# Attention and routed experts on one core: loads of x group by group, ones by a memset, a third group normed on VectorE, a later clear

## What is computed

```python
xn = _layernorm(x, axis=-1)
x = x + _L0_attn_ref(xn, Wqkv, Wproj, bproj) + _L0_ffn_ref(xn, gate_w, gate_b, w1, b1, w2, b2)
# attention: 16 heads of 8, rotary q and k, causal within a window of 64, softmax, times v, projected
# experts: gates = xn @ gate_w.T + gate_b; the 2 best of 8, softmax over the two;
#          gelu(xn @ w1[e] + b1[e]) @ w2[e] + b2[e], weighted
```

## Time and profile before

| | us |
|---|---|
| median of 3 runs | 841.19 (840.72 to 841.76) |
| the profiled execution | 844.36 |
| its span | 842.5 |
| mean granted clock of TensorE | 0.943 of full speed |

### The profile page before, as it was taken

The page is one execution under the profiler, slowest core; times in us unless marked ns, Lnnn a source line. Parts: engine busy times, 40 slices in busy tenths (PEclk is TensorE's granted clock), DMA queues, the critical chain, the costliest instruction groups (busy, mean ns, idle before and its releaser), DMA issues.

```text
span 842.5 us, 26905 instructions
## 1 busy us (share of the span) xinstructions
PE 696.1 (83%) x10234; PEld 541.9 (64%) x10238; DVE 493.3 (59%) x1382; ACT 359.2 (43%) x681; POOL 408.4 (48%) x566
## 2 busy tenths in 40 slices
PE   6567888767877778778777979999999999998776
PEld 3455666545555545545554669899998988986554
DVE  6589877886556656556545834444444444454764
ACT  1435764424344433344334533444343434444443
POOL 2675331015555555545554135666666655664334
PEclk9899998879999999899989989999999999999987
DMA  9587767344564745654664777888888877883878
GB/s 259 148 204 198 174 155 185 90 136 131 153 175 133 192 124 132 158 153 122 153 167 122 184 195 217 221 232 225 229 229 219 213 212 218 223 228 94 231 237 249
DMA packets 213079, 154.15 MB, mean 183 GB/s; under 512 B 32560, under 2 KB 192944, under 8 KB 212952
## 3 DMA queue, kind: packets, MB, share of 16 engines
q1 hardware_dynamic: 199032, 131.41, 60.6%
q0 software_dynamic: 8640, 17.97, 6.2%
q10 hardware_dynamic: 5280, 3.06, 1.3%
HBM read 97.93 MB, written 54.34 MB: 181 GB/s over the span
## 4 chain that ended last, share of the span: by engine, by line
PE 24%; DVE 21%; issue 19%; DMA 10%; another core or an unknown queue 8%; POOL 7%; SPq 7%; ACT 2%; ACTq 0%; DVEq 0%; POOLq 0%
DVE mx L885 8%; POOL chosen_y L1135 6%; PE ps L614 4%; DMA chosen_y<-xn,to 4%; PE ps L561 3%; DMA xn<-in_b 3%; PE ps L554 2%; SPq L352 2%; PE ps L665 2%; PE ps L678 2%; PE ps L598 2%; POOL xn L1146 1%; PE ps L642 1%; PE ps L591 1%
## 5 line engine op out<-in xcount | busy, mean ns | idle before, releaser
L885 DVE TENSOR_REDUCE mx<-ps 128x8 f32<-128x1024 f32 x128 | 156.6, 1223 | 145.9 <-remote 74.2
L1053 ACT ACTIVATE PT<-ps 128x1024 f32<-128x1024 f32 x128 | 131.0, 1023 | 236.7 <-PE ps L598 199.0
L1129 POOL DMA_INDIRECT slots_x<-xn,pos x128 | 126.5, 988 | 130.6 <-DVE mx L885 96.1
L1074 ACT ACTIVATE hb<-ps,b1b 128x256 f32<-128x256 f32 x284 | 116.5, 470 | 162.6 <-issue 93.3
L1135 POOL DMA_INDIRECT chosen_y<-xn,to x142 | 137.9, 971 | 48.9 <-issue 30.3
L678 PEld LDWEIGHTS ps<-xn,hb 128*128 128x128 f32 x1136 | 138.4, 192 | 3.7
L678 PE MATMUL ps<-xn,hb 128*128 128x128 f32 x1136 | 138.5, 275 | 0.0
L665 PE MATMUL ps<-xn 128*128 128x256 f32 x568 | 136.1, 383 | 0.0
L614 PE MATMUL ps<-PT,V 128*32 128x64 f32 (+1 forms) x3072 | 104.6, 258 | 16.2 <-issue 11.2
L665 PEld LDWEIGHTS ps<-xn 128*128 128x128 f32 x568 | 103.5, 192 | 11.4
L937 DVE TENSOR_TENSOR to<-eq,cf_s 128x2 int32<-128x2 f32 x71 | 11.9, 168 | 135.6 <-DMA chosen_y<-xn,to 97.8
(11 more groups left out here) (130 smaller groups left out, 931.1 us busy)
## 6 DMA issues: line engine op xcount, KB each, us to landing
xn<-in_w SPq DMA_DIRECT2D x142, 256.0 KB
QK<-stack SPq DMA_DIRECT2D x128, 192.0 KB
stack<-sp SPq DMA_DIRECT2D x64, 192.0 KB
xn<-slots_x SPq DMA_DIRECT2D x71, 132.0 KB
stack<-sp SPq DMA_DIRECT2D x64, 128.0 KB
xn<-chosen_y SPq DMA_DIRECT2D x32, 256.0 KB, 4.3
xn<-in_b SPq DMA_DIRECT2D x71, 64.0 KB
stack<-sp SPq DMA_DIRECT2D x64, 64.0 KB
```

The source lines that it names most:

```text
L885: e.tensor_reduce(mo[:, :, :, c, t], ps[:, 0:2, :].rearrange("p g (h k) -> p g h k", k=P), AX.X, ALU.max, negate=True).then_inc(v_mx, 1)
L1053: e.activation(PT[:, u % 2, :], ps[:, 2:4, :].rearrange("p c k -> p (c k)"), ACT.Exp, scale=SCALE).then_inc(a_exp, 1)
L1074: e.activation(hb[:, s, c, :], ps[:, 2 * s + c // 2, (c % 2) * SL:(c % 2 + 1) * SL], ACT.Gelu, bias=b1b[:, i % NW, c:c + 1]).then_inc(a_ge ...
L1129: e.indirect_dma_start(out=Xs, out_offset=bass.IndirectOffsetOnAxis(ap=pos[:, n, u:u + 1], axis=0), in_=xn[:, u, :], in_offset=None).then_ ...
```

## The change

The first four loads of x are issued at the start, the others one by one, group 4 + k at q = -22 + 4 k, and SP issues them where the list says. The clear goes from the front to q = -12. The ones are no longer copied by SP: GpSimd sets the whole k half of `QK` (four buffers of 2048 bf16 per partition) to 1.0 by a memset before its cast, and the first reads into `QK` and the first transposed scores wait for that. The loads of the weights are put in another order, the values' and the gate's weights with a semaphore of their own, the bias with another, for which the gate's addition now waits. Group 2 is normed wholly on VectorE, as groups 0 and 1.

```diff
-    order = [("warm", 16), ("clear",)]
+    order = [("warm", 16)] + [("xload", g) for g in range(4)]
...
-        for g in range(2, NG):
+        for g in range(3, NG):
             d = FIRST + 4 * (g - 1) - q
             order.extend(("apply", g, j) for j, at in enumerate((4, 3, 2, 2, 1, 0)) if d == at)
-        if q == FIRST + 3:
-            order.append(("ones",))
+        if q - FIRST in range(0, 4 * (NG - 4), 4):
+            order.append(("xload", 4 + (q - FIRST) // 4))
+        if q == FIRST + 10:
+            order.append(("clear",))
...
         @block.sync
-            for g in range(NG):
-                e.dma_start(xr[:, GR[g]:GR[g + 1], :], xv[:, GR[g]:GR[g + 1], :]).then_inc(d_x[g], 16)
             for what, *a in ORDER:
-                if what == "ones":
-                    e.wait_ge(p_cb, 1)
-                    for n in range(NQ):
-                        for g in range(2):
-                            e.dma_start(QK[64 * g + 48:64 * g + 51, n, 1, :].rearrange("p (r c) -> p r c", c=P),
-                                        onesb[0:3, :].unsqueeze(1).broadcast_to((3, 16, P))).then_inc(d_one, 16)
+                if what == "xload":
+                    g = a[0]
+                    e.dma_start(xr[:, GR[g]:GR[g + 1], :], xv[:, GR[g]:GR[g + 1], :]).then_inc(d_x[g], 16)
...
                     if b >= NQ:
                         e.wait_ge(e_st, 4 * (b - NQ) + 4)
+                    else:
+                        e.wait_ge(p_init, 4)
...
         @block.tensor
-                    e.wait_ge(d_q, LOADS_Q)
+                    e.wait_ge(d_q, 16)
...
-                        e.wait_ge(d_one, 32 * NQ)
+                        e.wait_ge(p_init, 4)
...
         @block.vector
-                    if g >= 2:
+                    if g >= 3:
                         continue
...
-                    e.wait_ge(d_q, LOADS_Q)
+                    e.wait_ge(d_wv, LOADS_WV)
...
                     e.wait_ge(e_vg, n + 1)
+                    e.wait_ge(d_gb, 16)
...
         @block.scalar
+            e.dma_start(wv_f, wqkv[:, 256:384]).then_inc(d_wv, 16)
+            e.dma_start(gw_s[:], gate_w).then_inc(d_wv, 16)
             e.dma_start(wq_s[:], wqkv[:, 0:256]).then_inc(d_q, 16)
-            e.dma_start(wv_f, wqkv[:, 256:384]).then_inc(d_q, 16)
-            e.dma_start(gw_s[:], gate_w).then_inc(d_q, 16)
-            e.dma_start(gb_s[:], gate_b.partition_broadcast(P)).then_inc(d_q, 16)
+            e.dma_start(gb_s[:], gate_b.partition_broadcast(P)).then_inc(d_gb, 16)
...
         @block.gpsimd
             e.memset(ones8[:], 1.0).then_inc(p_init, 1)
+
+            e.memset(QK[:, :, 1, :], 1.0).then_inc(p_init, 1)
             e.wait_ge(d_cb, 16)
             e.tensor_copy(cb_s[:], cb_f).then_inc(p_cb, 1)
...
-                if what == "norm" and a[0] >= 2:
+                if what == "norm" and a[0] >= 3:
```

More of the change, by code:

```diff
@@ L286, in attention_moe_kernel @@
         d_g = [semaphore(f"d_g{i}") for i in range(NF)]
-        d_o, d_one = semaphore("d_o"), semaphore("d_one")
+        d_o, d_wv, d_gb = semaphore("d_o"), semaphore("d_wv"), semaphore("d_gb")
         e_xt, e_vg, e_rt, e_qk, e_qt, e_sc, e_mt, e_st = (semaphore("e_" + n) for n in (
@@ L308, in attention_moe_kernel @@
         block = ctx.enter_context(nc.Block())
-        LOADS_Q = 4 * 16
+        LOADS_WV = 2 * 16
         LOADS_C = 16
@@ L323, in xn_ready @@
         def xn_ready(u):
-            if u < GR[2]:
+            if u < GR[3]:
                 return v_xn, u + 1
-            g, j = divmod(u - GR[2], 6)
+            g, j = divmod(u - GR[3], 6)
             return (p_xn, 3 * g + ON_POOL.index(j) + 1) if j in ON_POOL else (a_xn, 3 * g + ON_ACT.index(j) + 1)
@@ L979, in _ @@
                     g, u = a[0], GR[a[0]] + a[1]
-                    e.wait_ge(p_nrm, PNRM * (g - 1))
+                    e.wait_ge(p_nrm, PNRM * (g - 2))
                     e.activation(xn[:, u, 0:P], xr[:, u, :], ACT.Identity, bias=nb[:, u:u + 1],
@@ L1091, in _ @@
                     n1, n2 = nb[:, u0:u1], mv[:, u0:u1, 0]
-                    k = PNRM * (g - 2)
-                    e.wait_ge(v_nrm, 24 + 3 * (g - 1))
+                    k = PNRM * (g - 3)
+                    e.wait_ge(v_nrm, 36 + 3 * (g - 2))
                     for _ in range(3):
@@ L1123, in _ @@
                         e.wait_ge(d_z, 16 * (1 + NE))
-                        e.wait_ge(v_xn, GR[2])
-                        e.wait_ge(a_xn, (NT - GR[2]) // 2)
-                        e.wait_ge(p_xn, (NT - GR[2]) // 2)
+                        e.wait_ge(v_xn, GR[3])
+                        e.wait_ge(a_xn, (NT - GR[3]) // 2)
+                        e.wait_ge(p_xn, (NT - GR[3]) // 2)
                     if n == 0 or u % 2:
```

## The result

| | before | changed |
|---|---|---|
| median, four runs each | 841.48 us (840.72 to 842.35) | 852.52 us (849.52 to 857.58) |
| the profiled execution | 844.36 us | 854.76 us |
| its span | 842.5 us | 852.9 us |
| mean granted clock of TensorE | 0.943 | 0.925 |

The ratio is 1.0137, with an interval of 1.0081 to 1.0193: slower, by 11.0 us where the prediction had 5.0. 852.5 lies outside the range of 839.0 to 848.4. The sign and the first half of the mechanism were right; the size was not.

The account below looks back on a forecast made before the run. The prediction took the start to be bound by a chain of waits, then VectorE's work. The turn's +3.2 us and the clear's +1.8 gave +5.0 on 841.19, so 846.2 us, with an 8-in-10 range of 839.0 to 848.4.

Parts of the forecast that it names:

- The gap of 3.9 us: Before the first rotated q and k turn: VectorE ready 3.9 us before the queued values' store landed, the most winnable there.
- Memset held in full: At group 0's first guess: GpSimd's memset, 6.9 us by elements, holds VectorE's step until it ends, +4.66 us.
- Rivals 1 to 3: At VectorE's group-0 step: memset holds nobody, clear hidden, 839.3 (0.17); likewise, clear paid, 841.1 (0.13); memset by bytes, 842.7/840.9 (0.12).
- The cast: On GpSimd directly behind the memset: falls into group 0's norm, +0.82 us, and no longer stalls group 1's, -0.50.
- The 1.38 us: In VectorE's start: its wait for the gate's bias goes, worth 0 to 1.38 us.
- Third group, 3.34 us: Ahead of the rotation of q and k: norming group 2 on VectorE adds 3.34 us; GpSimd and ScalarE end no wait.
- The turn: TensorE's first turn of rotated q and k, forecast to start near 29.95 instead of 26.79, +3.2 us.
- From there the order is that of before: From the turn to the first scores: same steps wait for SP, ScalarE and GpSimd, so nothing is added.
- the spread loads of x: On SP's queue: loads of groups 4 to 10, one per four steps, land in time; cost 0, bound 1 us.
- The clear, +1.8: At step -12, ahead of pair 1's write: the clear delays scores 4 by 1.8 us, bounds 0 and 3.9.
- Carried through: Behind the start: a microsecond lost or won before 48 us reaches the end, since every engine runs one fixed order.
- The sum: Over the whole kernel: 3.2 us at the turn plus 1.8 for the clear, +5.0 us.

Follow-up runs that it names:

- e8: Changed kernel with the memset as half as many f32 elements, put first, and the clear behind the store of values 1; 759.44 us, ratio 1.0000.
- e2: Kernel before with only the GpSimd memset of QK in place of SP's copied ones; 759.12 us, ratio 1.0023.
- e4: Changed kernel with group 2's Newton rounds and rows back on GpSimd and ScalarE; 762.51 us, ratio 1.0056.
- e6: Changed kernel with the memset as 4096 f32 elements, put first on GpSimd, and V's clearing moved behind the cast; 760.22 us, ratio 1.0013.
- e9: Changed kernel with short early memset, early clear, group 2 on GpSimd and ScalarE (its row later), zero products, x loads reordered; 754.74 us, ratio 0.9947.
- e10: Kernel before with loads of x in parts, weights' loads reordered and the clear behind the store of values 1; 758.47 us, ratio 1.0009.
- e3: Changed kernel with the clear issued behind the store of values 1 instead of at step -12; 763.33 us, ratio 1.0042.
- e11: Kernel before with loads of x in parts, weights' loads reordered and the clear at step -12; 759.08 us, ratio 1.0005.
- e5: Changed kernel with twelve products of zeros in TensorE's gap before the turn; 765.35 us, ratio 1.0086.

## Why the prediction was right or wrong

**The gap of 3.9 us.** Right for the changed kernel: with the queue short its turn follows VectorE's sum, and once the memset is out of the way it comes at 24.85 (e8), 1.9 us before the old one with a group more on VectorE. What the text did not see is that 3.9 us is VectorE's reserve alone: while GpSimd norms group 2, ScalarE's way to the same turn had only 1.6 (e2, e4).

**Memset held in full.** Right, in mechanism and size: the memset took 6.92 us against 6.9, the held step 4.68 against some 4.8. It moves what follows by 4.51 us; the sum's 4.66 counts the step's own 0.17 once too often. The Trainium skill, "SBUF — State Buffer", Who interferes with whom, counts any GpSimd instruction against a VectorE one that uses both ports; this trace agrees, for an instruction that only writes, with 4.68 us where 0.17 is usual. "VectorE: DVE Perf Modes" (Trainium skill), Zero memsets, states the count by elements for VectorE; of GpSimd the runs here show the same, 6.92 us for 8192 and 3.51 for 4096 elements of equal bytes. Rivals 1 to 3 fall with these rows. The 0.87 ns an element that the prediction gives the cast is not in its row: 0.82 us for 768 elements are 1.07. That the cost would vanish with an earlier, shorter memset was not in the text, and was worth 4.5 us at the turn (e6).

**The cast, and the weights.** Nearly: 0.82 was forecast, 0.63 came (1.74 less 1.11), but through the late landing of the constants and not from its place behind the memset. The 1.38 us were counted as gone only in the rivals, rightly, as in the held case the wait lay under the hold.

**Third group, 3.34 us.** The row was read rightly, the counterpart was not: the text says that GpSimd and ScalarE end no wait in the new order, but with group 2 left to them ScalarE's L981 would stand in front of the values' copy (e4: 1.2 to 1.3 us net). It doesn't enter the sum for the kernel as changed, where VectorE paid all of it. What the text lacked is its echo at the routing.

**The turn.** +2.68 us against +3.2.

**"From there the order is that of before".** This step failed. The order was that of before, the time of two of its parts was not: in the changed kernel's first profile 2.7 us were added between the turn and the first scores. 2.1 of them lie in front of the read of pair 0, where TensorE was granted 0.50; the other 0.7 are the read itself, 6.3 to 7.1 us from its issue to the scores in every trace with a load of x right in front of it, and 5.9 and 5.5 in before and e2. The prediction had the spread loads of x at 0 (bound 1 us); why the read takes longer isn't shown, since it took 6.2 and 6.6 in e9, where that load is gone. I had the granted clock of before in the earlier trace rows (0.66 and 0.74 in the start, 1.00 from 40 to 50 us) and treated it as a constant of the stage. In the changed kernel TensorE stands idle for all of 24 to 28 us (0.00 busy, before 1.21) and comes back at 0.50, where it stays to 36 (the kernel before comes back at 0.50 too, and has 0.74 from 28 to 32). It would be easy to call that the cause. The other traces don't bear it out as a rule: from 20 to 40 us e10, whose turn came after 4.97 us of idling, had 0.68, and the kernel before, with 6.72 us of idling, 0.83; the changed kernel itself had 0.57, 0.83 and 0.57 in its three profiles. Shown is what a low grant costs there, about 2 us at the first maxima (53.5 and 53.7 against 51.6, and the two groups of the sixteen traces), and that the changed kernel met it in two of three profiles; why, isn't.

**The clear, +1.8.** Right in place and nearly in size: 2.1 us in the changed kernel's marks (+5.4 to +7.5), 2.3 to 2.6 by e3, 1.3 by e11 against e10.

**Carried through.** Right to scores 28 (+7.9 from 8 to 28). Behind it the routing adds 1.5 us (+9.4 at scores 32), which no part of the prediction had; and the end has +10.4.

**The sum.** By its own steps: 2.68 (turn) + 2.06 (clock) + 0.66 (read) + 2.15 (clear) + 0.35 (from scores 4 to 28) + 1.50 (routing) + 1.00 (behind scores 32) = 10.4 us of span, against 5.0. On the two other chips the same kernel costs 4.5 and 7.4 us. The first of these is the forecast's size, but that doesn't bear the forecast's sum out: the execution whose marks are known took 765.47 us, 7.8 over the median of before, and it has +5.9 at scores 28 and +7.8 at scores 32. Of an execution near the median there is no trace. The range was too narrow above because it had nothing for the clock, for the read and for the routing. The clock alone doesn't make the miss: without its 2.1 us the time would be about 850.5 (an estimate), still above 848.4. A clock term was needed all the same: the four runs of the changed kernel alone spread over 8 us (849.52 at a clock of 0.931, 857.58 at 0.906), about 3 us for each hundredth.

**What stays open.** Why the grant differs between executions of one kernel; why the first read of the stack takes 0.7 us longer; why the last store of values takes half a microsecond or more longer with group 2 on VectorE; where behind scores 32 the last 1.0 us arises; how much of the first chip's longer time belongs to its scatter stage, which is 75 us longer there in the changed kernel; none of the later runs was on such a chip.

## What to carry to other kernels

Before work is moved to an engine that "is idle anyway", look for what runs beside it on VectorE: here a GpSimd memset cost by its elements and held a step of VectorE until it ended, so writing bf16 ones as half as many f32 elements, before VectorE had anything to do, took the hold away. The reserve in front of a wait is a number for each engine that leads to it (here 3.9 us for VectorE, 1.6 for ScalarE). Don't price TensorE's products in a thinly used stage by one profile of before: take the rows at the lower clock for the upper bound of the range. And a large transfer with no deadline belongs where nothing dependent stands behind it on its queue.

## What the runs showed of the hardware

- A GpSimd instruction that reads nothing (the memset) made a VectorE step on 4 elements per partition last 4.5 to 4.7 us, elsewhere 0.17, in every kernel that had it in its place (changed, e2, e3, e4, e5).
- The kernel before took 841.5 us on one chip and 757.5 to 758.1 on four others. The changed kernel's marks up to scores 28 agree between two of the chips to 0.4 us at a like clock; most of its difference (75 us) lies in the stretch with the indirect scatters.
- The same instructions at the same time of the program were granted 0.68 and 0.50 of TensorE's clock in two executions, worth 1.8 us at the first maxima.
- With twelve products of zeros at the front of the gap the clock was 0.79 from 28 to 36 us, but 0.83 from 40 to 60 (0.97 and 0.92 without them); the time did not fall.
- With a transfer of 924 KB in front, the issuing of six small writes took 6.4 us and not 3.1.
